# Attention over edges: TensorE adds up the slots of all five groups, and four engines run in a new order

## The chip, the core and the metric

The kernel runs on one core of a Trainium2 chip. The metric is the device time of one execution in microseconds. A core has five engines with queues of their own: TensorE (PE in the profile), VectorE (DVE), ScalarE (ACT), GpSimd (POOL) and SyncE (SP), which here only issues transfers. They meet through semaphores. TensorE adds into PSUM; everything else lies in SBUF.

## What is computed

Four graph layers over 3125 nodes with 16 features and 103125 edges, sorted by their target. Only the fourth, an attention over the edges of each node, is touched:

```python
w_m = (efeat @ W_msg + b_msg).reshape(E, in_f, -1)
w_a = (efeat @ W_attn + b_attn).reshape(E, in_f, -1)
h_src = feat[src][:, :, None]
e1 = w_m * h_src
e2 = w_a * h_src
seg_max = jax.ops.segment_max(e2, dst, num_segments=N)
ex = jnp.exp(e2 - seg_max[dst])
denom = jax.ops.segment_sum(ex, dst, num_segments=N)
attn = ex / denom[dst]
ft = jax.ops.segment_sum(e1 * attn, dst, num_segments=N)
return ft.sum(axis=1)
```

## The kernel before

Edges stand in rows of four slots that share a target node; empty slots are filled. Each of the 128 partitions owns 220 such rows in sequence. Five rows on every partition are five groups, and 5 x 4 = 20 slots are a block (`BLK`); there are 44 blocks (`BLOCKS`). One slot of one block holds, per partition, 512 numbers: for each of 16 input and 16 output features the attention value `e2` and the message `e1`. Two blocks are in flight, in the buffers `e[0]` and `e[1]`, named by `u`.

For each block the work is this. GpSimd gathers the source features of the 20 slots into `hs[u]`, one indirect transfer per slot. TensorE forms one product per slot (line 1872) from the edge features `ef[u]`, which SyncE loads. The product lies in PSUM (`wps`) and is multiplied by the gathered features into `e[u]`: VectorE does slots 0 to 3, 8 to 11 and 16 to 19, four at a time (line 1981), ScalarE slots 4 to 7 and 12 to 15 (line 1942, 16 instructions per slot). VectorE takes the maximum over the four slots of a group (lines 2001 and 2003), carries it from group to group with `up` (line 2010) and back with `down` (line 2015), so that the rows of one node share one shift, and subtracts it (line 2028, one instruction per group). ScalarE takes the exponentials (line 1952, one per group) and that of `scale` (line 1948), the factor by which the state of the block before is rescaled. VectorE weighs the messages with the exponentials (line 2046, one per group). The four slots of a group are then summed: for groups 0 to 3 TensorE adds them with an identity matrix in PSUM (line 1894, four matmuls, eight records in the trace), for group 4 VectorE halves (line 2055) and quarters (line 2060). Then VectorE carries the state over from the block before (line 2067) and accumulates group after group (lines 2081 and 2083). SyncE stores the shifts (line 1785) and the states (line 1790).

The order is written out by hand on each engine. VectorE's `block_step(b)` weighs and accumulates block b - 1, finds the shifts of block b and subtracts them, and multiplies its slots of block b + 1. ScalarE's `turn(b)` multiplies its slots of block b + 1 and takes the exponentials of block b: in the order scale, then groups 4 to 0, all between slots 6 and 7. TensorE's `period` forms the products of block b + 1 between the sums of block b - 1. A turn of ScalarE starts when the gathers of its block have landed and when TensorE has summed group 1 of the block whose buffer it is about to overwrite. TensorE forms a product for ScalarE only when ScalarE has read the one two before, since there are two banks for these, and those for VectorE when the four banks have been read. GpSimd starts the gathers of a block when ScalarE and VectorE have read all of the block two before. ScalarE's loop holds two turns, and the first of the two begins with a table load.

Of the kernel before, what the change touches and what calls it, by code (L numbers as in the profile page):

```python
# [27 lines left out]
F = 16  # L28
# [31 lines left out]
SLOTS = 4  # L60
# [1632 lines left out]
def attention_edges(nc, io, keep, d, sem, lastrow):  # L1693
# [10 lines left out]
    EARLY, LATE1, LATE3 = (4, 5, 6), (7,), (12, 13, 14, 15)  # L1704
    BYACT = [*EARLY, *LATE1, *LATE3]
# [4 lines left out]
    BYPE = 4  # L1710
    SUM_READ = (3, 4, 6, 7)
    SUM_DONE = (2, 2, 3, 4)
    NM = 2
    assert BG == 5 and SLOTS == 4 and sorted(ORDER) == list(range(BLK))
    with ExitStack() as ctx:
        def sb(name, shape, dt=F32):
# [20 lines left out]
        a_w, a_mult, a_read_v, a_read_s, a_sub, a_exp, a_weighed, a_sum, a_halved, a_acc, a_shift, a_last, a_step, a_go = (  # L1737
            sem("a_" + s) for s in "w mult read_v read_s sub exp weighed sum halved acc shift last step go".split())
# [31 lines left out]
        with nc.Block() as block:  # L1770
# [97 lines left out]
            def _(pe):  # L1868
# [20 lines left out]
                def summed(u, b, g):  # L1889

                    pe.wait_ge(a_weighed, b * BYPE + (g + 1))
                    pe.wait_ge(a_acc, b * BG + SUM_READ[g])
                    for c in range(SLOTS):
                        ins = nc.tensor.matmul(sums[:, g % 2, :], ident[:, :], e[u][:, g * SLOTS + c, :],  # L1894
                                               start=(c == 0), stop=(c == SLOTS - 1))
                    ins.then_inc(a_sum, 1)

                def period(u, b, before):
# [17 lines left out]
                    for_dve(u, b, 2, NV + 2)  # L1916
                    for_act(u, b, (13, 14, 15))
# [10 lines left out]
                for g in (1, 0, *range(2, BYPE)):  # L1928
                    summed(0, BLOCKS - 2, g)
                for g in (1, 0):  # L1930
                    summed(1, BLOCKS - 1, g)

            @block.scalar
            def _(act):
# [10 lines left out]
                def exponentials(u, b):  # L1945

                    act.wait_ge(a_sub, b * (BG + 1) + 1)
                    nc.scalar.activation(scale[u][:, :], scale[u][:, :], ACT.Exp).then_inc(a_exp, 1)
                    for n, g in enumerate(reversed(range(BG))):
                        act.wait_ge(a_sub, b * (BG + 1) + (n + 2))  # L1950
                        e2 = all_e2(u, g, g + 1)[:, 0, :, :]
                        nc.scalar.activation(e2, e2, ACT.Exp).then_inc(a_exp, 1)  # L1952
# [3 lines left out]
                multiply(0, 0, [*EARLY, *LATE1])  # L1956
                act.wait_ge(a_first[3], FIRST[3])
                multiply(0, 0, LATE3)
# [14 lines left out]
                exponentials(1, BLOCKS - 1)  # L1973

            @block.vector
            def _(dve):
# [64 lines left out]
                def weigh(v, u, b):  # L2041

                    dve.wait_ge(a_exp, (b + 1) * (BG + 1))
                    for g in range(BG):
                        pair = e[u][:, g * SLOTS:(g + 1) * SLOTS, :].rearrange("p c (i a o) -> p (c i) a o", a=2, o=F)
                        ins = nc.vector.tensor_tensor(pair[:, :, 1, :], pair[:, :, 0, :], pair[:, :, 1, :], ALU.mult)  # L2046
                        if g < BYPE:
                            ins.then_inc(a_weighed, 1)
                        else:
                            v.add(ins)  # L2050
# [12 lines left out]
                def carry(v, u, b, stored):  # L2063

                    dve.wait_ge(a_acc, b * BG + BG)
# [4 lines left out]

                def accumulate(v, u, b, g, by_pe=BYPE):

                    if g < by_pe:
                        total = sums[:, g % 2, :]
                        dve.wait_ge(a_sum, b * BYPE + (BYPE + SUM_DONE[g]))
                    else:
                        total = e[u][:, g * SLOTS, :]
                        v.wait(v.n)
# [10 lines left out]
                dve.sem_inc(a_sum, BYPE)  # L2089
                dve.sem_inc(a_halved, 1)  # L2090
# [21 lines left out]
                largest(v, 0, 0, 0, 3, len(EARLY) + len(LATE1))  # L2112
# [5 lines left out]
                for g in reversed(range(BG)):  # L2118
                    subtract(0, g)
# [4 lines left out]
                def block_step(v, u, b, i, more=True):  # L2124
# [5 lines left out]
                    weigh(v, w, b - 1)  # L2130
                    masks(v, u, b)
# [326 lines left out]
```

## Time and profile before

| | before |
|---|---|
| median of 3 runs | 2714.13 us (2713.15 to 2716.22) |
| profiled execution | 2713.4 us |
| its span, first to last instruction | 2711.7 us |
| VectorE busy | 2260.6 us (83%) |
| TensorE busy, matmuls | 1949.8 us (72%) |
| ScalarE busy | 1747.4 us (64%) |
| GpSimd busy | 1324.2 us (49%) |

The shares are over the whole execution, which has stages with different limits. The attention loop fills the time from about 1116 us to 2643 us; before it lie the other layers, behind it some 70 us in which the rows of each node are fetched and divided. A timeline row gives the start in us from the span's first instruction, the busy time of the instructions merged in it, their number, and in brackets the engine's idle time before them and what ended it. The recorded end of a VectorE instruction lies a little behind the start of the next where that does not depend on it, so costs are read from start to start.

### The profile page before, as it was taken

To read this page: it belongs to the slowest core of one execution; us is meant where nothing else is said; L and a number is where in the kernel's file an instruction comes from. 1 tells how busy PE (TensorE), PEld (TensorE's weight loads), DVE (VectorE), ACT (ScalarE), POOL (GpSimd) and SP (SyncE) were. 2 spreads that over 40 slices of the span, in tenths; PEclk is the share of its full clock that TensorE was granted. 3 is DMA by queue.
4 is the path that set the end of the run, shared out by engine and by line. 5 is a ranking of instruction groups with operands and counts; after the bars stand their busy time and mean duration, and the time that the engine had idled before them with its cause. 6 is when DMAs were issued, how large, how long until landed. Compare 5 with 4: busy or idle time off the path is not lost. (4 is left out here: it accounts for less than half of the span.)

```text
span 2711.7 us, 35345 instructions
## 1 busy us (share of the span) xinstructions
PE 1949.8 (72%) x7015; PEld 998.3 (37%) x7016; DVE 2260.6 (83%) x3915; ACT 1747.4 (64%) x6869; POOL 1324.2 (49%) x1141
## 2 busy tenths in 40 slices
PE   0688888898788978447777777776777777777760
PEld 0344444455444543223333333333333333333320
DVE  7799999313587861269999999999999999999996
ACT  6577777112211112378888888888888888888844
POOL 5000000404551000477777777777777777777705
PEclk8899999887898988668888788888888888888885
DMA  3000000203787652222222223333222332222214
GB/s 71 6 0 0 0 0 0 95 1 120 257 287 240 197 185 71 38 46 85 85 85 85 85 87 89 89 89 87 85 85 85 86 87 86 86 86 86 76 65 118
DMA packets 125233, 238.09 MB, mean 88 GB/s; under 512 B 40438, under 2 KB 68766, under 8 KB 119418
## 3 DMA queue, kind: packets, MB, share of 16 engines
q1 hardware_dynamic: 83289, 189.23, 21.0%
q0 software_dynamic: 41888, 48.19, 8.3%
q8 instruction: 26, 0.43, 0.1%
q14 instruction: 30, 0.24, 0.0%
HBM read 94.14 MB, written 143.02 MB: 87 GB/s over the span
## 5 line engine op out<-in xcount | busy, mean ns | idle before, releaser
L1831 POOL DMA_INDIRECT hs<-h_table,gix x860 | 1084.3, 1261 | 347.3 <-issue 241.8
L1942 ACT ACTIVATE e<-wps,hs 128x32 f32<-128x32 f32 x5632 | 1014.7, 556 | 92.1 <-DMA hs<-h_table,gix 66.6
L1894 PE MATMUL slot_sums<-e,ident 128*128 128x512 f32 x1392 | 773.3, 708 | 18.9 <-DVE states L2081 11.8
L1872 PE MATMUL wps<-w_terms,ef 72*128 72x512 f32 x880 | 409.3, 559 | 451.9 <-ACT e L1942 272.1
L1894 PEld LDWEIGHTS slot_sums<-e,ident 128*128 128x128 f32 x1392 | 318.4, 232 | 395.2 <-issue 362.3
L1872 PEld LDWEIGHTS wps<-w_terms,ef 72*128 72x128 f32 x880 | 178.6, 211 | 643.4 <-ACT e L1942 344.0
L529 ACT CAST edges<-acc 128x400 f32 x600 | 295.2, 492 | 100.1 <-PE acc L516 73.6
L512 PE MATMUL acc<-q_hot,lo_hot 128*128 128x400 bf16 x1200 | 306.6, 337 | 53.7 <-DVE q_hot L486 51.8
L1981 DVE TENSOR_TENSOR e<-wps,hs 128x2048 f32<-128x2048 f32 x132 | 301.9, 2287 | 39.6 <-PE wps L1872 25.6
L554 POOL DMA_INDIRECT got<-in_edge_rows,start x64 | 65.0, 1015 | 543.1 <-POOLq L467 415.9
L486 DVE TENSOR_SCALAR q_hot<-qcol,qT 128x400 bf16<-128x400 bf16 x1200 | 290.8, 321 | 0.3 <-PE acc L516 0.2
L1952 ACT ACTIVATE e<-e 128x1024 f32<-128x1024 f32 x220 | 248.1, 1136 | 55.3 <-DVE e L2028 45.0
L2028 DVE TENSOR_TENSOR e<-e,shifts 128x1024 f32<-128x1024 f32 x220 | 256.8, 1219 | 0.0
L2046 DVE TENSOR_TENSOR e<-e 128x1024 f32<-128x1024 f32 x220 | 253.5, 1220 | 0.0
L1293 PE MATMUL acc<-edges,msg_parts 128*128 128x448 bf16 x1050 | 216.9, 363 | 13.0 <-DMA msg_parts<-msg 13.0
L516 PE MATMUL acc<-edges,ident_b 128*128 x600 | 202.5, 338 | 0.2 <-ACT edges L529 0.2
L1322 ACT CAST efT_high<-tr 128x512 fp32r<-128x512 f32 x56 | 32.8, 586 | 244.2 <-DMA ef_high<-efT_high 201.4
L512 PEld LDWEIGHTS acc<-q_hot,lo_hot 128*128 128x128 bf16 x1200 | 130.8, 140 | 93.6 <-DVE q_hot L486 68.9
L1293 PEld LDWEIGHTS acc<-edges,msg_parts 128*128 128x128 bf16 x1050 | 105.4, 100 | 105.7 <-DMA msg_parts<-msg 13.4
L2001 DVE TENSOR_TENSOR pairs<-e 128x1536 f32<-128x1536 f32 x88 | 130.8, 1487 | 8.3 <-ACT e L1942 8.3
L482 DVE TENSOR_TENSOR lo_hot<-lane,loT 128x1280 bf16<-128x1280 bf16 x120 | 98.7, 823 | 16.1 <-PE acc L516 11.9
L2010 DVE SCALAR_TENSOR_TENSOR shifts<-shifts,mk 128x256 f32<-128x256 f32 x220 | 106.2, 483 | 4.8
(384 smaller groups left out, 2006.7 us busy)
## 6 DMA issues: line engine op xcount, KB each, us to landing
rows_state<-states SPq DMA_DIRECT2D x43, 1280.0 KB, 4.6
rows_shift<-shifts SPq DMA_DIRECT2D x44, 640.0 KB, 3.0
ef<-ef_high SPq DMA_DIRECT2D x88, 180.0 KB
ef<-ef_low SPq DMA_DIRECT2D x88, 180.0 KB
got_order<-edges_order SPq DMA_DIRECT2D x56, 256.0 KB, 2.9
ef_high<-efT_high SPq DMA_DIRECT2D x56, 256.0 KB, 3.1
ef_low<-efT_low SPq DMA_DIRECT2D x56, 256.0 KB, 3.3
hs<-h_table,gix POOLq DMA_INDIRECT x880, 3.8
```

The costliest lines, as they stand in the source:

```text
L486: ins = nc.vector.tensor_scalar(q_hot[:, k % HOTS, s, :], qcol[:, :], qT[:, s, at], None, ALU.is_equal)
L512: nc.tensor.matmul(total, lo_hot[:, k // HOTS % 2, :, k % HOTS * 2 + s], q_hot[:, k % HOTS, s, :], start=(s == 0), stop=False)
L529: nc.scalar.copy(edges[:, :, bass.ds(s16, W)], acc[:, k % BANKS, 0:QW].rearrange("p (t w) -> p t w", w=W)).then_inc(taken, 1)
L1293: ins = nc.tensor.matmul(acc[:, at, 0:CW], parts[:, f, k, a, :], edges[:, k, at * CW:(at + 1) * CW], start=(n == 0), stop=(n == 3 * TILES ...
L1831: nc.gpsimd.indirect_dma_start(out=hs[u][:, s, :], out_offset=None, in_=d["h_table"], in_offset=bass.IndirectOffsetOnAxis(ap=gix[u][:, s:s ...
L1872: nc.tensor.matmul(wps[:, bank, :], ef[u][:, c, g * P:(g + 1) * P], w[:, :], start=True, stop=True).then_inc(a_mult, 1)
L1894: ins = nc.tensor.matmul(sums[:, g % 2, :], ident[:, :], e[u][:, g * SLOTS + c, :], start=(c == 0), stop=(c == SLOTS - 1))
L1942: ins = nc.scalar.mul(e[u][:, s, at], wps[:, bank, at], hs[u][:, s, f:f + 1])
L1952: nc.scalar.activation(e2, e2, ACT.Exp).then_inc(a_exp, 1)
L1981: nc.vector.tensor_tensor(e[u][:, s0:s1, :].rearrange("p s (i c) -> p (s i) c", c=2 * F), wps[:, 0:s1 - s0, :].rearrange("p s (i c) -> p ( ...
L2028: nc.vector.tensor_tensor(e2, e2, bc(shift(u, g), 1, SLOTS), ALU.subtract).then_inc(a_sub, 1)
L2046: ins = nc.vector.tensor_tensor(pair[:, :, 1, :], pair[:, :, 0, :], pair[:, :, 1, :], ALU.mult)
```

## The change

TensorE now sums all five groups of every block but the last, and the halving and quartering on VectorE remain only behind the last block. Groups go in the order 0 to 4 everywhere, where the subtracts and exponentials had gone from 4 to 0. Each weigh waits for its own exponential and not for all six; `scale` has a semaphore of its own (`a_scaled`). VectorE spreads the weighs over the step: 0 and 1, the first maxima, 2, the carry, the second maxima, accumulation 0, weigh 3, the upward shifts, weigh 4. ScalarE takes one exponential at a time between its slots, and scale and groups 3 and 4 after slot 15. The two banks for sums alternate from block to block as well.

```diff
-    ORDER = [4, 5, 0, 1, 2, 3, 6, 7, 8, 9, 10, 11, 12, 16, 17, 18, 19, 13, 14, 15]
+    ORDER = [0, 1, 2, 3, 4, 5, 6, 7, 12, 8, 9, 10, 11, 13, 16, 17, 18, 19, 14, 15]
...
-                    pe.wait_ge(a_weighed, b * BYPE + (g + 1))
-                    pe.wait_ge(a_acc, b * BG + SUM_READ[g])
+                    pe.wait_ge(a_weighed, b * BG + (g + 1))
+                    pe.wait_ge(a_acc, b * BG + (BG + g - 1))
...
+                    for_dve(u, b, 0, NV)
+                    add(0)
+                    for_act(u, b, (4, 5))
                     add(1)
-                    for_act(u, b, (4,))
-                    add(0)
-                    for_act(u, b, (5,))
-                    for_dve(u, b, 0, NV)
+                    add(2)
                     for_act(u, b, (6,))
-                    add(2)
-                    for_act(u, b, (7,))
+                    add(3)
+                    for_act(u, b, (7, 12))
                     for_dve(u, b, 1, NV + 1)
-                    add(3)
-                    for_act(u, b, (12,))
+                    add(4)
+                    for_act(u, b, (13,))
                     for_dve(u, b, 2, NV + 2)
-                    for_act(u, b, (13, 14, 15))
+                    for_act(u, b, (14, 15))
...
-                    act.wait_ge(a_sum, b * BYPE + 1)
-                    multiply(1 - u, b + 1, EARLY)
-                    exponentials(u, b)
-                    multiply(1 - u, b + 1, LATE1)
-                    act.wait_ge(a_sum, b * BYPE + 4)
-                    multiply(1 - u, b + 1, LATE3)
+                    act.wait_ge(a_sum, b * BG + 2)
+                    multiply(1 - u, b + 1, (4, 5, 6))
+                    exponential(u, b, 0)
+                    multiply(1 - u, b + 1, (7,))
+                    act.wait_ge(a_sum, b * BG + 4)
+                    multiply(1 - u, b + 1, (12,))
+                    exponential(u, b, 1)
+                    multiply(1 - u, b + 1, (13,))
+                    exponential(u, b, 2)
+                    multiply(1 - u, b + 1, (14, 15))
+                    rescaled(u, b)
+                    exponential(u, b, 3)
+                    exponential(u, b, 4)
...
+                def weigh(u, b, g):
+
+                    dve.wait_ge(a_exp, b * BG + (g + 1))
...
+                    dve.wait_ge(a_scaled, b + 1)
                     dve.wait_ge(a_acc, b * BG + BG)
...
-                    weigh(v, w, b - 1)
-                    masks(v, u, b)
+                    weigh(w, b - 1, 0)
+                    weigh(w, b - 1, 1)
...
-                    largest(v, u, b, 0, 3, len(EARLY) + len(LATE1))
+                    largest(v, u, b, 0, 3, SLOTS)
+                    weigh(w, b - 1, 2)
+                    carry(v, w, b - 1, i * 16 + 16 * u)
+                    masks(v, u, b)
                     found = largest(v, u, b, 3, BG, NS)
+                    accumulate(v, w, b - 1, 0)
+                    weigh(w, b - 1, 3)
                     v.wait(found)
-                    for g in range(2):
+                    for g in range(4):
                         v.wait(up(v, u, g))
-                    shifted = up(v, u, 2)
-                    halve(w, 4).then_inc(a_halved, 1)
-                    v.wait(shifted)
-                    shifted = up(v, u, 3)
-                    carry(v, w, b - 1, i * 16 + 16 * u)
-                    v.wait(shifted)
                     shifted = up(v, u, 4)
-                    v.wait(shifted - 1)
-                    accumulate(v, w, b - 1, 0)
+                    weigh(w, b - 1, 4)
                     accumulate(v, w, b - 1, 1)
...
+                    subtract(u, 0)
+                    next_block(0)
+                    accumulate(v, w, b - 1, 2)
+                    subtract(u, 1)
+                    subtract(u, 2)
+                    next_block(1)
+                    subtract(u, 3)
+                    accumulate(v, w, b - 1, 3)
                     subtract(u, 4)
-                    next_block(0)
-                    for g in reversed(range(4)):
-                        subtract(u, g)
-                    accumulate(v, w, b - 1, 2)
-                    next_block(1)
-                    dve.wait_ge(a_halved, b + 1)
-                    quarter(v, w, 4)
-                    accumulate(v, w, b - 1, 3)
                     accumulate(v, w, b - 1, 4)
-                    dve.wait_ge(a_acc, b * BG + BG)
                     next_block(2)
```

On VectorE the first half of a step stood like this before (L2046 weighs, L1988 copies the marks, L2001 and L2003 are the maxima, L2010 the upward shifts, L2055 the halving, L2067 the carry, L2081 accumulation 0):

```order
L2046 TENSOR_TENSOR e<-e 128x64x16 x5
L1988 COPY mk<-marks 128x10
L2001 TENSOR_TENSOR pairs<-e 128x1536
L2003 TENSOR_TENSOR shifts<-pairs 128x768
L2001 TENSOR_TENSOR pairs<-e 128x1024
L2003 TENSOR_TENSOR shifts<-pairs 128x512
L2010 SCALAR_TENSOR_TENSOR shifts<-shifts,mk 128x256 x3
L2055 TENSOR_TENSOR e<-e 128x1024
L2010 SCALAR_TENSOR_TENSOR shifts<-shifts,mk 128x256
L2067 TENSOR_TENSOR states<-states,scale 128x512
L2010 SCALAR_TENSOR_TENSOR shifts<-shifts,mk 128x256
L2081 TENSOR_TENSOR states<-states,slot_sums 128x512
```

It now stands like this (L2053 weighs, L2009 and L2011 are the maxima, L2072 the carry, L1996 copies the marks, L2087 is accumulation 0, L2018 the upward shifts):

```order
L2053 TENSOR_TENSOR e<-e 128x64x16 x2
L2009 TENSOR_TENSOR pairs<-e 128x1536
L2011 TENSOR_TENSOR shifts<-pairs 128x768
L2053 TENSOR_TENSOR e<-e 128x64x16
L2072 TENSOR_TENSOR states<-states,scale 128x512
L1996 COPY mk<-marks 128x10
L2009 TENSOR_TENSOR pairs<-e 128x1024
L2011 TENSOR_TENSOR shifts<-pairs 128x512
L2087 TENSOR_TENSOR states<-states,slot_sums 128x512
L2053 TENSOR_TENSOR e<-e 128x64x16
L2018 SCALAR_TENSOR_TENSOR shifts<-shifts,mk 128x256 x5
L2053 TENSOR_TENSOR e<-e 128x64x16
```

The halving is gone, the weighs are apart, the carry has come ahead of the upward shifts, and these stand in one row.

On ScalarE a turn, here the one behind the loop, stood like this before (L1942 multiplies, 16 instructions to a slot, L1948 is the exponential of scale, L1952 that of a group; the last row belongs to what follows the turn):

```order
L1942 ACTIVATE e<-wps,hs 128x32 x48
L1948 ACTIVATE scale<-scale 128x256
L1952 ACTIVATE e<-e 128x64x16 x5
L1942 ACTIVATE e<-wps,hs 128x32 x80
L1948 ACTIVATE scale<-scale 128x256
```

It now stands like this (L1939 multiplies, L1951 is the exponential of a group, L1945 that of scale):

```order
L1939 ACTIVATE e<-wps,hs 128x32 x48
L1951 ACTIVATE e<-e 128x64x16
L1939 ACTIVATE e<-wps,hs 128x32 x32
L1951 ACTIVATE e<-e 128x64x16
L1939 ACTIVATE e<-wps,hs 128x32 x16
L1951 ACTIVATE e<-e 128x64x16
L1939 ACTIVATE e<-wps,hs 128x32 x32
L1945 ACTIVATE scale<-scale 128x256
L1951 ACTIVATE e<-e 128x64x16 x2
```

Scale has moved from behind the third slot to behind the eighth, and two of the five exponentials come after it.

On TensorE a period in the loop began like this before (L1894 is a sum, L1872 a product; the rows without a tile work out what the next one waits for):

```order
L1894 MATMUL slot_sums<-e,ident 128x512 x4
L1886 ISA
L1872 MATMUL wps<-w_terms,ef 128x512
L1891 REGISTER_ALU
L1892 REGISTER_ALU
L1894 MATMUL slot_sums<-e,ident 128x512 x4
L1886 REGISTER_ALU
L1872 MATMUL wps<-w_terms,ef 128x512
L1877 ISA
L1872 MATMUL wps<-w_terms,ef 128x512 x4
```

It now begins like this (L1869 is a product, L1891 a sum):

```order
L1869 MATMUL wps<-w_terms,ef 128x512 x4
L1888 ISA
L1889 REGISTER_ALU
L1891 MATMUL slot_sums<-e,ident 128x512 x4
L1883 ISA
L1869 MATMUL wps<-w_terms,ef 128x512
L1883 REGISTER_ALU
L1869 MATMUL wps<-w_terms,ef 128x512
L1888 REGISTER_ALU
L1889 REGISTER_ALU
L1891 MATMUL slot_sums<-e,ident 128x512 x4
```

Four products for VectorE have come to the front, and two products stand between the first two sums where one stood.

## Rows read from the trace of the kernel before

**Rows 1.** SyncE's queue: the store of the shifts in steps 1 and 43.

```profile
1210.49 0.37 SPq L1785 DMA_DIRECT2D rows_shift<-shifts  x1
...
2617.72 0.33 SPq L1785 DMA_DIRECT2D rows_shift<-shifts  x1
```

**Rows 2.** Busy time in 42 steps: PE, PEld, DVE, ACT, POOL; clock, DMA, GB/s.

```profile
1210.50:2617.70 1407.20, 1012.95 (x2179) 470.79 (x2178) 1385.50 (x1552) 1213.66 (x5612) 1033.07 (x814) 0.82 0.29 84
```

**Rows 3.** Timeline of VectorE in one step: weighs to accumulation 1, then its end.

```profile
1929.68 5.76 DVE L2046 TENSOR_TENSOR e<-e 128x1024 f32<-128x1024 f32 x5
...
1935.43 1.75 DVE L2001 TENSOR_TENSOR pairs<-e 128x1536 f32<-128x1536 f32 x1
...
1938.10 1.22 DVE L2001 TENSOR_TENSOR pairs<-e 128x1024 f32<-128x1024 f32 x1
...
1940.08 1.53 DVE L2010 SCALAR_TENSOR_TENSOR shifts<-shifts,mk 128x256 f32<-128x256 f32 x3
1941.52 1.22 DVE L2055 TENSOR_TENSOR e<-e 128x1024 f32<-128x1024 f32 x1
1942.66 0.48 DVE L2010 SCALAR_TENSOR_TENSOR shifts<-shifts,mk 128x256 f32<-128x256 f32 x1
1943.05 0.68 DVE L2067 TENSOR_TENSOR states<-states,scale 128x512 f32<-128x512 f32 x1
...
1944.05 0.68 DVE L2081 TENSOR_TENSOR states<-states,slot_sums 128x512 f32<-128x512 f32 x1
1944.77 0.75 DVE L2083 SCALAR_TENSOR_TENSOR states<-states,mk,slot_sums 128x512 f32<-128x512 f32 x1
1945.43 2.05 DVE L2015 SCALAR_TENSOR_TENSOR shifts<-shifts,mk 128x256 f32<-128x256 f32 x4
...
1958.65 0.68 DVE L2060 TENSOR_TENSOR e<-e 128x512 f32<-128x512 f32 x1
1959.46 0.75 DVE L2083 SCALAR_TENSOR_TENSOR states<-states,mk,slot_sums 128x512 f32<-128x512 f32 x1
1960.25 0.75 DVE L2083 SCALAR_TENSOR_TENSOR states<-states,mk,e 128x512 f32<-128x512 f32 x1
1961.12 2.29 DVE L1981 TENSOR_TENSOR e<-wps,hs 128x2048 f32<-128x2048 f32 x1
```

**Rows 4.** Timeline of TensorE: first two sums, shortest and longest of 43 pairs.

```profile
1430.15 4.81 PE L1894 MATMUL slot_sums<-e,ident 128*128 128x512 f32 x8
...
1435.03 3.60 PE L1894 MATMUL slot_sums<-e,ident 128*128 128x512 f32 x8
...
2536.02 6.61 PE L1894 MATMUL slot_sums<-e,ident 128*128 128x512 f32 x8
...
2542.70 3.60 PE L1894 MATMUL slot_sums<-e,ident 128*128 128x512 f32 x8
```

**Rows 5.** Timeline of ScalarE: the first turn, and two turns of the loop.

```profile
1181.18 0.80 ACT L1948 ACTIVATE scale<-scale 128x256 f32<-128x256 f32 x1
1181.49 5.21 ACT L1952 ACTIVATE e<-e 128x1024 f32<-128x1024 f32 x5
...
1907.72 1.28 ACT L1942 ACT_TABLE_LOAD   x1 [3.47 <-DMA hs<-h_table,gix]
...
1923.37 14.37 ACT L1942 ACTIVATE e<-wps,hs 128x32 f32<-128x32 f32 x80
1941.12 8.68 ACT L1942 ACTIVATE e<-wps,hs 128x32 f32<-128x32 f32 x48 [3.38 <-DMA hs<-h_table,gix]
```

**Rows 6.** Timeline of GpSimd: a batch of 20 gathers and the next one's first.

```profile
1905.12 1.52 POOL L1831 DMA_INDIRECT hs<-h_table,gix  x1 [2.34 <-ACT e L1942]
...
1926.10 0.94 POOL L1831 DMA_INDIRECT hs<-h_table,gix  x1 [0.30 <-issue]
...
1934.29 1.97 POOL L1831 DMA_INDIRECT hs<-h_table,gix  x1 [0.30 <-issue]
1938.55 1.58 POOL L1831 DMA_INDIRECT hs<-h_table,gix  x1 [2.29 <-ACT e L1942]
```

More of the change, by code:

```diff
@@ L1736, in attention_edges @@
         sums = ctx.enter_context(nc.psum_tensor("slot_sums", [P, 2, 2 * CH], F32))
-        a_w, a_mult, a_read_v, a_read_s, a_sub, a_exp, a_weighed, a_sum, a_halved, a_acc, a_shift, a_last, a_step, a_go = (
-            sem("a_" + s) for s in "w mult read_v read_s sub exp weighed sum halved acc shift last step go".split())
+        a_w, a_mult, a_read_v, a_read_s, a_sub, a_exp, a_scaled, a_weighed, a_sum, a_acc, a_shift, a_last, a_step, a_go = (
+            sem("a_" + s) for s in "w mult read_v read_s sub exp scaled weighed sum acc shift last step go".split())
         a_marks, a_x, a_terms, a_split = sem("a_marks"), sem("a_x"), sem("a_terms"), sem("a_split")
@@ L1927, in _ @@
                         period(u, i * 2 + (2 + u), i * 2 + u)
-                for g in (1, 0, *range(2, BYPE)):
+                for g in range(BG):
                     summed(0, BLOCKS - 2, g)
-                for g in (1, 0):
+                for g in range(BY_PE_LAST):
                     summed(1, BLOCKS - 1, g)
@@ L1943, in multiply, with rescaled, exponential @@
                         ins.then_inc(a_read_s, 1)
-                def exponentials(u, b):
+                def rescaled(u, b):
                     act.wait_ge(a_sub, b * (BG + 1) + 1)
[L1948 to L1952, printed above, removed]
+                    nc.scalar.activation(scale[u][:, :], scale[u][:, :], ACT.Exp).then_inc(a_scaled, 1)
+                def exponential(u, b, g):
+                    act.wait_ge(a_sub, b * (BG + 1) + (g + 2))
+                    e2 = all_e2(u, g, g + 1)[:, 0, :, :]
+                    nc.scalar.activation(e2, e2, ACT.Exp).then_inc(a_exp, 1)
                 act.sem_inc(a_read_s, NS)
                 act.wait_ge(a_first[1], FIRST[1])
-                multiply(0, 0, [*EARLY, *LATE1])
+                multiply(0, 0, (4, 5, 6, 7))
                 act.wait_ge(a_first[3], FIRST[3])
-                multiply(0, 0, LATE3)
+                multiply(0, 0, (12, 13, 14, 15))
                 def turn(u, b, gathered):
                     act.wait_ge(a_gather[1 - u], gathered)
-                    act.wait_ge(a_sum, b * BYPE + 1)
-                    multiply(1 - u, b + 1, EARLY)
-                    exponentials(u, b)
-                    multiply(1 - u, b + 1, LATE1)
-                    act.wait_ge(a_sum, b * BYPE + 4)
-                    multiply(1 - u, b + 1, LATE3)
+                    act.wait_ge(a_sum, b * BG + 2)
[11 more added lines that the diff above has]
+                    exponential(u, b, 4)
                 with act.Fori(0, BLOCKS // 2 - 1) as i:
@@ L1972, in _ @@
                 turn(0, BLOCKS - 2, BLOCKS // 2 * GM)
-                exponentials(1, BLOCKS - 1)
+                rescaled(1, BLOCKS - 1)
+                for g in range(BG):
+                    exponential(1, BLOCKS - 1, g)
             @block.vector
@@ L2039, in group @@
                     return e[u][:, g * SLOTS:(g + 1) * SLOTS, :].rearrange("p c n -> p (c n)")
[L2041 to L2050, printed above, removed]
+                def weigh(u, b, g):
+                    dve.wait_ge(a_exp, b * BG + (g + 1))
+                    pair = e[u][:, g * SLOTS:(g + 1) * SLOTS, :].rearrange("p c (i a o) -> p (c i) a o", a=2, o=F)
+                    nc.vector.tensor_tensor(pair[:, :, 1, :], pair[:, :, 0, :], pair[:, :, 1, :], ALU.mult
+                                            ).then_inc(a_weighed, 1)
                 def halve(u, g):
@@ L2117, in _ @@
                 rescale(0)
-                for g in reversed(range(BG)):
+                for g in range(BG):
                     subtract(0, g)
@@ L2180, in _ @@
                 block_step(v, 1, BLOCKS - 1, BLOCKS // 2 - 1, more=False)
-                weigh(v, 1, BLOCKS - 1)
+                for g in range(BG):
+                    weigh(1, BLOCKS - 1, g)
                 carry(v, 1, BLOCKS - 1, 16 * (BLOCKS // 2))
                 v.wait(v.n)
-                for g in range(2, BG):
+                for g in range(BY_PE_LAST, BG):
                     v.then(halve(1, g))
```

23 lines of the change are left out of this document (10 added, 13 removed).

## The prediction

> **What bounds the kernel now.** The stage that the diff touches is a loop of 44 blocks, one step each on every engine. I read the stores of the shifts first, since SyncE issues one per step: from 1210.49 to 2617.72 us lie 42 steps [rows 1], so a step takes 1407.23 / 42 = 33.51 us, and 42 x 33.51 of the execution's 2713.4 us is this loop. The chain that ended last says nothing here, as it follows only the work behind the loop. Next the busy time of the engines in that stretch [rows 2]: VectorE 1385.5 of 1407.2 us (98.5%), ScalarE 1213.7 (86%), TensorE 1013.0 (72%), GpSimd 1033.1 (73%). Then VectorE's own timeline of one step [rows 3]: no row of it has an idle time before it; each instruction starts where the one before lets it. The others do wait: ScalarE 3.4 us per step for gathered rows [rows 5], GpSimd 2.3 us for ScalarE [rows 6]. So VectorE's sum is the step, and what leaves it is worth its full time until something else is late. How late the others are is the real question.
>
> **Part one: VectorE's step.** Starts are read from the timeline [rows 3]; an instruction that does not wait for the one before starts about 0.08 us before that one's recorded end, one that does wait about 0.03 after.
> The halving of group 4 goes: 1941.52 to 1942.66, 1.14 us. The quartering goes: 0.68 busy, 0.60 by the start-to-start rule.
> The accumulations 3 and 4 each had to wait for their forerunner, 0.79 and 0.87 to the next start; spaced out as they now are, each costs what accumulation 1 costs before the downs, 0.66. That saves 0.13 + 0.21 = 0.34. Accumulation 0 no longer stands right ahead of 1: 0.72 becomes 0.60, 0.12 saved.
> Against this, the five upward shifts now stand in a row. Before, three took 1.44 to the start of the halving, then 0.39 and 0.40 beside other work, 2.23 in all; four dependent ones at 0.52 and one at 0.40 make 2.48, 0.25 more.
> Sum: -1.14 - 0.60 - 0.34 - 0.12 + 0.25 = -1.95. VectorE alone would need 33.51 - 1.95 = 31.56 us. Weighs, subtracts, multiplies, maxima and downs are moved, not changed in number; moving costs nothing as long as VectorE never waits.
>
> **Part two: what VectorE now waits for.** The change turns one wait for six exponentials into one per group, and ScalarE's scale now comes behind slot 15. So I follow one chain, with time 0 at the first weigh of a step. Weigh 0 ends at 1.2; TensorE, which has made products 0 to 3 in that time, starts sum 0 at about 1.3. Sum 0, products 4 and 5 and sum 1 follow. TensorE had the like before, two sums with one product between, in the same place behind a quiet stretch. The shortest such pair in the 43 steps took 1430.15 to 1438.63, 8.48 us, the longest 2536.02 to 2546.30, 10.28 [rows 4]; their middle is 9.4, and a product more costs no more than one of a sum's eight records, 3.60 / 8 = 0.45; I take half of that, 0.23. So sum 1 is there at 1.3 + 9.4 + 0.23 = 10.9. In each pair the first sum is the long one, 4.81 and 6.61 against 3.60: the granted clock averages 0.82 over the stretch [rows 2], and the lower of its two levels falls on the first sum.
> ScalarE's turn starts there, as it must not overwrite slots 4 and 5 before sum 1. In every second turn a table load of 1.28 comes first [rows 5]. Then eight slots at 14.37 / 5 = 2.87 make 23.0, three exponentials at about 1.0 (five in 5.21 where nothing held them) 3.0, the scale 0.31 to the next start. Scaled is there 26.3 later: at 37.2, or 38.5 with the load.
> VectorE wants it at the carry: two weighs at 1.14, the first maximum (1935.43 to 1938.10) 2.67, another weigh 1.14, so 6.1 into the next step, 31.56 + 6.1 = 37.65 on this clock. The plain turn is 0.4 early, the one with the load 0.9 late. Two steps take 2 x 31.56 + 0.9 = 64.0, so a step 32.0. The price of this new wait is bounded below by 0 (TensorE wholly at its higher level, below) and above by the longest pair: sum 1 at 11.8, one turn 1.75 late and the other 0.45, a mean of 1.1 and a step of 32.65. I take 0.45, the middle of the rows.
> Slot 15, which the second maximum needs at 31.56 + 6.9, is read about 0.35 before the scale; that wait comes after the carry and adds nothing once the carry has waited. Exponentials 3 and 4 end 1 and 2 us behind the scale, and weighs 3 and 4 come 3.3 and 7 us behind the carry: covered. Sums 2 to 4 wait for accumulations 0 to 2, and product 6 is queued behind sum 2 on TensorE: sum 2 starts at 10.9, ends near 14.5, and ScalarE wants product 6 at 10.9 + 5.7: covered. Products 8 to 11 and 16 to 19 stand behind sums 3 and 4 only where these are done 2 us ahead of VectorE's multiplies: covered at the higher level; at the lower a multiply waits 1 to 2 us, which happens now and then and is in the upper bound.
>
> **Part three: edges.** The 42 steps give 42 x (33.51 - 32.0) = 63.4 us. In the last step the subtracts and accumulations behind the last store of shifts save the quartering and the waits, 0.9. The first step waits for gathers and ScalarE before and after, which I cost at nothing, plus or minus 1 us. The loads of features still follow product 15, and SyncE's two stores still follow the downs and accumulation 4, in the same order. So 2713.4 - 63.4 - 0.9 = 2649.1. The median of the runs is 0.7 above the profiled execution; I take 2649.
>
> **A rule weighed.** Rows show that after a quiet stretch the first sum takes 4.81 to 6.61 us and the one behind it 3.60 [rows 4]. The Trainium skill (TensorE: Matmul & The Clock Gate, "Part 1: The HAM clock gate") says that the slow clock is the resting state and that activity lifts it. By that rule TensorE's fifth sum could keep the higher level on; the trace agrees that the level rises within the first sum, while whether four more matmuls suffice no row shows.
>
> **Rivals.**
> *VectorE alone.* If both sums ran at the higher level, the pair would take 2 x 3.60 + 2 x 0.23, or 7.7, sum 1 would be there at 9.0 and even the turn with the load would scale at 36.6, before 37.65. The step is 31.56, the time 2713.4 - 42 x 1.95 - 0.9 = 2630.6. For it: more work on TensorE. Against it: no pair of the 43 came near 7.7, and the quiet stretch stays, as products 14 and 15 and then 0 to 3 wait for ScalarE and VectorE.
> *The gathers bind.* A batch of 20 gathers takes 1905.12 to 1936.26, 31.1 us, and the next starts 0.8 after ScalarE's last slot (1923.37 + 14.37 = 1937.74 to 1938.55) [rows 5, 6]; ScalarE gets its rows 4.9 after the last one (1936.26 to 1941.12). One buffer's round trip is thus ScalarE's turn up to slot 15 (26.0, or 27.3 with the load) + 0.8 + batch + 4.9 over two steps. A gather takes 0.94 us, but 1.97 while VectorE weighs [rows 6]; the halving that goes frees one of them, so the batch is 30.2 and the trip 63.2, 31.6 a step: just covered. Were two more gathers of each batch caught by VectorE's newly scattered instructions, the batch would be 32.2 and the step 32.6: 2713.4 - 42 x 0.91 - 0.9 = 2674. The Trainium skill (SBUF — State Buffer, "Who interferes with whom") says that a VectorE instruction with two SBUF inputs blocks a GpSimd instruction that reads SBUF for its whole length; the slow gathers agree. The page infers that making a DMA's descriptors is not caught by it, and there the measured 1.97 decides.
> *Slower.* TensorE at its lower level through both sums: a record at that level takes twice as long, so the pair about 2 x 6.9 + 0.9 = 14.7, sum 1 is there at 16.0, and where both turns bind a step is sum 1 + 26.3 + 0.64 (half the load) - 6.1 = 36.8, 42 x 3.3 = 139 more: 2852. It decides from sum 1 at 12.7, where that sum reaches 33.51, a pair of 11.1. For it: sum 0 follows a quiet stretch. Against: in both pairs shown the second sum is already at 3.60.
> *No gain.* If not VectorE but the gathers' round trip set the step before (31.1 + 4.9 + 30 + 0.8 = 66.8 of 67.0), the halving would be worth nothing: 2713. Against it: the trip is shortened too, as two exponentials and the scale leave ScalarE's turn ahead of slot 15.
>
> **How the numbers follow.** The forecast, a step near 32.0 (2638 to 2660): 0.50. VectorE alone (2628 to 2638): 0.20. Gathers, or TensorE's sums later than the middle (2660 to 2700): 0.22. No gain: 0.03. Slower: 0.05. The range from 2629 to 2674 takes in both ends of the carry's wait and half of the third case, about 0.82. A difference under 0.2%, 5 us, cannot be told from none. Faster 0.92, same 0.03, slower 0.05.
>
> **What would show it.** After: stores of shifts 32.0 apart, in pairs of unequal length; VectorE idle about 0.9 us ahead of the carry in every second step, released by ScalarE's scale, and nowhere else; ScalarE's wait at a turn's start ended by sum 1, no longer by gathers; pairs of sums of 8.5 to 10.5 us. Stores 31.6 apart and no idle time on VectorE mean the first rival; ScalarE still waiting for gathers the second. The prediction is wrong if VectorE waits at a multiply or at a maximum, or if its instructions themselves grow longer.

## The result and the profile after

The changed kernel takes 2664.4 us (median of 4 runs, 2663.5 to 2668.7) against 2715.0 (2713.2 to 2716.2) in runs taken beside it: ratio 0.9817, interval 0.9800 to 0.9834. It is faster, as forecast; the gain is 51 us where 65 were forecast. The time lies inside the range, but not in the band of the forecast (2638 to 2660, chance 0.50); it lies in that of the gathers or of sums later than the middle (2660 to 2700, 0.22). The profiled execution took 2664.25 us, its span 2662.5.

SyncE's stores of the shifts, as in [rows 1]; first the one in step 1, then three in a row, last the one in step 43:

```profile
1210.80 0.37 SPq L1782 DMA_DIRECT2D rows_shift<-shifts  x1
...
1922.49 0.38 SPq L1782 DMA_DIRECT2D rows_shift<-shifts  x1
...
1954.09 0.38 SPq L1782 DMA_DIRECT2D rows_shift<-shifts  x1
...
1987.35 0.38 SPq L1782 DMA_DIRECT2D rows_shift<-shifts  x1
...
2569.39 0.33 SPq L1782 DMA_DIRECT2D rows_shift<-shifts  x1
```

42 steps take 1358.59 us, 32.35 each, where they took 33.51. Short and long steps take turns, 31.60 and 33.26: two steps are 64.86 us, from about 1600 us on without drift. What lies around the 42 steps is 1305.7 us, before 1306.2.

The busy time in these steps, columns as in [rows 2], and then the waits from 1300 to 2500 us (engine, tile, line, what it waited for: us in total, times, longest):

```profile
1210.80:2569.39 1358.59, 1135.74 (x2515) 534.92 (x2514) 1311.48 (x1468) 1192.87 (x5617) 1072.48 (x813) 0.87 0.30 87
```

```profile
ACT L1939 <- PE slot_sums L1891: 83.1, 19, 5.0
...
ACT e L1939 <- DMA hs<-h_table,gix: 49.5, 19, 2.7
...
DVE states L2072 <- ACT scale L1945: 24.7, 19, 1.3
...
POOL hs L1828 <- ACT e L1939: 5.5, 18, 0.3
DVE e L1989 <- PE wps L1869: 2.7, 15, 0.2
```

VectorE's share fell from 98.5% to 96.5%. Its main wait is the carry's, for ScalarE's scale, 1.3 us in every second step; a small one, up to 0.2 us, stands at a multiply (L1989), for TensorE's products. Line L1939 is ScalarE's multiply; its two rows are the two kinds of turn, one with the table load, which sum 1 starts, one without, which waits for gathered rows. GpSimd waits for nothing longer than 0.3 us any more.

VectorE's timeline about the carry of a long step, which begins with a weigh at 1904.09; the first two rows end the step before it, in which the table was loaded:

```profile
1900.89 0.74 DVE L2089 SCALAR_TENSOR_TENSOR states<-states,mk,slot_sums 128x512 f32<-128x512 f32 x1
1901.80 2.29 DVE L1989 TENSOR_TENSOR e<-wps,hs 128x2048 f32<-128x2048 f32 x1 [0.18 <-PE wps L1869]
...
1909.02 1.22 DVE L2053 TENSOR_TENSOR e<-e 128x1024 f32<-128x1024 f32 x1
1911.56 0.69 DVE L2072 TENSOR_TENSOR states<-states,scale 128x512 f32<-128x512 f32 x1 [1.32 <-ACT scale L1945]
```

The carry stands at 7.47 after the first weigh, 1.40 later than in the short step, where it does not wait and stands at 6.07. And the accumulation ahead of the last multiply, of slots 16 to 19, takes 0.91 to the next start (1900.89 to 1901.80), where it takes 0.66 without a wait: 0.25 more, for the products. Together these are the 1.66 us between long and short steps. Then a turn with the load, in the step that begins at 1937.09: first TensorE's rows (products 0 to 3, then sum 0), then ScalarE's (table load, scale):

```profile
1937.14 2.07 PE L1869 MATMUL wps<-w_terms,ef 72*128 72x512 f32 x4 [0.87 <-DVE e L1989]
1939.02 5.88 PE L1891 MATMUL slot_sums<-e,ident 128*128 128x512 f32 x8
```

```profile
1948.91 1.28 ACT L1939 ACT_TABLE_LOAD   x1 [4.36 <-PE slot_sums L1891]
...
1974.83 1.37 ACT L1945 ACTIVATE scale<-scale 128x256 f32<-128x256 f32 x1
```

Sum 0 starts at 1.93, sum 1 lets ScalarE go at 11.8, and scaled is there at 39.1 after the first weigh; the next step begins at 31.85 and wants it 6.07 later, at 37.9.

GpSimd's gathers as a group from 1300 to 2500 us (count, busy us, mean ns of one, idle before), and the longest one:

```profile
L1828 POOL DMA_INDIRECT hs<-h_table,gix x741 | 975.2, 1316 | 225.8 <-issue 220.3 <-ACT e L1939 5.5
```

```profile
1937.85 4.08 POOL L1828 DMA_INDIRECT hs<-h_table,gix  x1 [0.30 <-issue]
```

A gather with the gap before it takes 1.316 + 0.305 = 1.62 us, 20 of them 32.4: the same as the mean step. So there are two suspects for the missing 14 us: the late scale, and GpSimd's full row.

### The profile page after: what moved, and what is told of

Read it like the earlier page. It is cut to its first block and busy times, and to the rows that moved or that the text cites. A ratio compares the mean times of both kernels' runs of the same rounds, so it can differ in the third digit from the quotient of the medians.

```text
span 2662.5 us, 36125 instructions
## 1 busy us (share of the span) xinstructions
PE 2079.0 (78%) x7359; PEld 1067.1 (40%) x7360; DVE 2184.5 (82%) x3829; ACT 1725.0 (65%) x6869; POOL 1365.8 (51%) x1141
## 5 line engine op out<-in xcount | busy, mean ns | idle before, releaser
L1828 POOL DMA_INDIRECT hs<-h_table,gix x860 | 1125.0, 1308 | 263.4 <-issue 257.3
L1939 ACT ACTIVATE e<-wps,hs 128x32 f32<-128x32 f32 x5632 | 1070.8, 681 | 97.8 <-DMA hs<-h_table,gix 49.5
L1891 PE MATMUL slot_sums<-e,ident 128*128 128x512 f32 x1736 | 913.0, 680 | 26.8 <-DVE states L2089 22.6
L1869 PE MATMUL wps<-w_terms,ef 72*128 72x512 f32 x880 | 374.5, 533 | 265.8 <-ACT e L1939 190.8
L1891 PEld LDWEIGHTS slot_sums<-e,ident 128*128 128x128 f32 x1736 | 382.3, 222 | 474.3 <-issue 411.7
L1869 PEld LDWEIGHTS wps<-w_terms,ef 72*128 72x128 f32 x880 | 179.8, 214 | 446.4 <-ACT e L1939 283.4
L1989 DVE TENSOR_TENSOR e<-wps,hs 128x2048 f32<-128x2048 f32 x132 | 301.3, 2283 | 42.4 <-PE wps L1869 39.9
L1951 ACT ACTIVATE e<-e 128x1024 f32<-128x1024 f32 x220 | 322.0, 1629 | 2.3 <-DVE e L2036 2.2
L2053 DVE TENSOR_TENSOR e<-e 128x1024 f32<-128x1024 f32 x220 | 263.9, 1217 | 0.0
L2036 DVE TENSOR_TENSOR e<-e,shifts 128x1024 f32<-128x1024 f32 x220 | 263.5, 1215 | 0.0
L1322 ACT CAST efT_high<-tr 128x512 fp32r<-128x512 f32 x56 | 32.8, 585 | 242.7 <-DMA ef_high<-efT_high 207.5
L2009 DVE TENSOR_TENSOR pairs<-e 128x1536 f32<-128x1536 f32 x88 | 130.6, 1484 | 1.9 <-ACT e L1939 1.9
L2089 DVE SCALAR_TENSOR_TENSOR states<-states,mk,slot_sums 128x512 f32<-128x512 f32 x173 | 127.6, 738 | 0.1
L2018 DVE SCALAR_TENSOR_TENSOR shifts<-shifts,mk 128x256 f32<-128x256 f32 x220 | 106.4, 484 | 6.3
```

Of the source, the lines that this page charges most:

```text
L1828: nc.gpsimd.indirect_dma_start(out=hs[u][:, s, :], out_offset=None, in_=d["h_table"], in_offset=bass.IndirectOffsetOnAxis(ap=gix[u][:, s:s ...
L1869: nc.tensor.matmul(wps[:, bank, :], ef[u][:, c, g * P:(g + 1) * P], w[:, :], start=True, stop=True).then_inc(a_mult, 1)
L1891: ins = nc.tensor.matmul(sums[:, (u + g) % 2, :], ident[:, :], e[u][:, g * SLOTS + c, :], start=(c == 0), stop=(c == SLOTS - 1))
L1939: ins = nc.scalar.mul(e[u][:, s, at], wps[:, bank, at], hs[u][:, s, f:f + 1])
L1989: nc.vector.tensor_tensor(e[u][:, s0:s1, :].rearrange("p s (i c) -> p (s i) c", c=2 * F), wps[:, 0:s1 - s0, :].rearrange("p s (i c) -> p ( ...
L2036: nc.vector.tensor_tensor(e2, e2, bc(shift(u, g), 1, SLOTS), ALU.subtract).then_inc(a_sub, 1)
```

## The experiments

**The load early.** One exponential at the head of ScalarE's loop.

```diff
                 with act.Fori(0, BLOCKS // 2 - 1) as i:
+                    nc.scalar.activation(early[:, :], ident[:, 0:1], ACT.Exp)
                     turn(0, i * 2, i * GM + GM)
```

> The changed kernel, with one exponential of a column of the identity matrix put at the top of ScalarE's loop, ahead of its waits, so that the loop's table load is over before sum 1 is there. Theory (the scale comes 1.4 to 1.66 us late to the carry in every second step, because of the 1.28 us load that stands behind the wait for sum 1): the load lies in the 4.36 us in which ScalarE waits anyway, the scale ends about 1.28 earlier, at 5.97 instead of 7.25 after the step's start, against 6.07 at which VectorE wants it. The long steps of 33.25 shrink to 31.6 to 31.8, the short ones stay at 31.59: 2664 - 20 x 1.5 = about 2634 us (2629 to 2640). Rival one (GpSimd's gathers, back to back, set the pace): no change, 2660 to 2666. Rival two (the low TensorE clock over sums 0 and 1 makes the lateness by itself): part of it, 2645 to 2655.

Measured: 2678.0 us, ratio 0.9857 (0.9832 to 0.9882), 14 us above the change (11 us by the two ratios). All three expectations missed. Waits and gathers:

```profile
ACT e L1940 <- DMA hs<-h_table,gix: 149.1, 37, 5.4
...
DVE states L2074 <- ACT scale L1946: 37.4, 34, 1.7
```

```profile
L1829 POOL DMA_INDIRECT hs<-h_table,gix x733 | 977.5, 1334 | 223.4 <-issue 217.6 <-ACT e L1940 5.8
```

Nearly every ScalarE turn now waits for gathered rows, and a step is 32.70 us: 20 x (1.334 + 0.305) = 32.8. With the load out of the way GpSimd's row is the bound, and it is longer than the 32.35 of the change.

**The kernel before with the load early**, the same line.

> The kernel before with the same early table load. Theory (VectorE's own row of work sets the 33.51 us step there, and ScalarE has room for its load): no change, 2712 to 2717 us. Rival (ScalarE's late exponentials already held VectorE before, so that the change gained by another way than VectorE's shorter row): a gain of 0.3 to 0.6 us in each step or in every second one, 2690 to 2707 us.

Measured: 2716.2 us, ratio 0.9997 (0.9987 to 1.0006): no change. ScalarE did not hold the step before.

**Halving back on VectorE**, the new orders kept.

```diff
-                    add(4)
...
+                    dve.wait_ge(a_weighed, b * BG)
+                    halved = v.add(halve(w, 4))
...
+                    quarter(v, w, 4)
                     accumulate(v, w, b - 1, 3)
```

> The changed kernel with its new orders kept, but group 4 halved and quartered on VectorE again, TensorE summing four groups. Theory (the gain comes from VectorE's work that was taken away, 1.14 + 0.60 us and the waits that stand with it, and the new order only makes room for it): the step is 31.59 + 1.74 + about 0.2 = 33.4 to 33.6 us without a wait for the scale, since VectorE wants it at the same point of its row while ScalarE has 1.8 us more: 42 x (33.5 - 32.42) more than the 2664 of the change, about 2709 us (2700 to 2716). Rival (the gain is the order's, the interleaved exponentials): 2660 to 2675 us.

Measured: 2719.8 us, ratio 1.0013 (1.0004 to 1.0023). Its 42 steps:

```profile
1216.46:2626.64 1410.18, 1032.59 (x2178) 492.86 (x2177) 1386.51 (x1552) 1193.94 (x5604) 972.55 (x813) 0.76 0.31 84
```

A step is 33.58 us and VectorE waits for none of the others, so all of the gain comes from the work taken off VectorE; the new orders alone give 33.58 a step against 33.51. The expected time was low: it set the step at 33.5 and the change's at 32.42, where 33.58 and 32.35 were measured (6 us), and it left out what lies ahead of the store in step 1, which comes 5.7 us later than in the change.

**Sixteen gathers.** This kernel leaves out four gathers of each block, so it does not do the whole computation; the same holds for all kernels below with 16 or 19.

```diff
+        GATHERED = (*range(4, BLK),)
...
-                    for s in range(BLK):
+                    for s in GATHERED:
...
+                    h0 = 8 if n == 0 and (not isinstance(b, int) or b > 0) else s0
...
-                        bc(hs[u][:, s0:s1, :].rearrange("p s i -> p (s i)"), 2, 2 * F), ALU.mult
+                        bc(hs[u][:, h0:h0 + 4, :].rearrange("p s i -> p (s i)"), 2, 2 * F), ALU.mult
```

> The changed kernel with 16 of 20 row gathers in every block: slots 0 to 3 are not gathered, and VectorE multiplies their products by the rows of slots 8 to 11 instead, so its work and its reads keep their size but the values of these slots are others. Theory (gathers don't set the pace, though GpSimd has no idle time left): the long steps stay at about 33.2, 2655 to 2666 us. Rival (the gathers, up to 4.08 us long now and without a pause between blocks, set the pace of the long steps): 2630 to 2645 us.

Measured: 2660.4 us, ratio 0.9797 (0.9781 to 0.9813). The 42 steps take 1358.84 us, as in the change; what is gained lies ahead of the first store, which comes at 1205.17 instead of 1210.80. Waits and gathers:

```profile
ACT L1940 <- PE slot_sums L1892: 96.3, 18, 5.4
...
ACT e L1940 <- PE slot_sums L1892: 40.4, 19, 2.2
...
DVE states L2074 <- ACT scale L1946: 25.7, 19, 1.4
```

```profile
L1829 POOL DMA_INDIRECT hs<-h_table,gix x591 | 716.3, 1212 | 484.6 <-ACT e L1940 308.1 <-issue 176.5
```

GpSimd has idle time again and ScalarE waits for sums alone, yet the carry waits as before: the late scale is enough by itself for 32.35 us a step.

**Both at once, and nineteen gathers with the load early.** The first is the load's line and the sixteen gathers together; the second differs from it by these (and `h0` is 1):

```diff
-        GATHERED = (*range(4, BLK),)
+        GATHERED = (*range(1, BLK),)
```

> The changed kernel with the early table load and 16 of 20 gathers in every block at once (slots 0 to 3 are not gathered and take the rows of slots 8 to 11, as in the kernel with sixteen gathers). New theory (two bounds stand within half a per cent of each other: ScalarE's late scale, which alone gives 64.86 us for two steps, and GpSimd's row of 20 gathers, 20 x (1.32 to 1.33 + 0.30) = 32.4 to 32.8 us a block, which alone gives 65 us and more): with both gone, VectorE's own row of 31.59 us is left in every step, with at most 0.1 for the scale, 2664 - 42 x (32.42 - 31.65) = 2632 us (2626 to 2640). Rival (the early load itself costs, or a third bound such as TensorE's clock stands behind both): 2650 us or more.

Measured: 2632.1 us, ratio 0.9677 (0.9661 to 0.9693). Its stores of the shifts in steps 1 and 43, and VectorE's one wait:

```profile
1205.70 0.37 SPq L1784 DMA_DIRECT2D rows_shift<-shifts  x1
...
2536.81 0.33 SPq L1784 DMA_DIRECT2D rows_shift<-shifts  x1
```

```profile
DVE states L2076 <- ACT scale L1947: 2.0, 5, 0.4
```

31.69 us a step: VectorE alone, but for these few waits. Neither edit gained in the loop by itself; together they take the time 32 us below the change's. That the forecast of 2632 was hit so closely is in part luck: it counted on 32 us in the loop, which gave 42 x (32.35 - 31.69) = 28, and the other 5 came from ahead of the store in step 1 (1205.70 instead of 1210.80).

> As the one before, but with 19 of 20 gathers: only slot 0 is not gathered, and slots 0 to 3 are multiplied by the rows of slots 1 to 4. New theory (GpSimd's back-to-back row sets the pace where the load is early): 19 x 1.64 = 31.1 us is less than VectorE's 31.59, so one gather fewer is enough and the time is 2630 to 2645 us. Rival (it is not the row's length but the lateness of what starts a block's gathers, so one fewer takes off one gather's 1.6 us at most once): 2655 to 2675 us.

Measured: 2639.6 us, ratio 0.9706 (0.9690 to 0.9722), 31.73 us a step. One gather fewer in each block is enough, which says that the length of GpSimd's row is what binds once the load is early.

**The scale sooner**, with 20 gathers and with 16.

```diff
-                    multiply(1 - u, b + 1, (14, 15))
                     rescaled(u, b)
+                    multiply(1 - u, b + 1, (14, 15))
```

> The changed kernel with the exponential of the scale moved ahead of ScalarE's multiplies of slots 14 and 15, all 20 gathers kept, load where it was. New theory (two bounds): the scale comes some 5.7 us sooner and the wait at the carry goes; the second maxima now wait for slots 14 and 15, about 0.5 later than the row wants them in the turn with the load, and the gathers stay at 32.4 us or more a block: 2660 to 2680 us, no gain. Rival (the late scale alone sets the pace): two steps 63.2 to 64.2, 2637 to 2658 us.

Measured: 2670.5 us, ratio 0.9823 (0.9805 to 0.9841), no gain. The carry's wait is gone; these stand in its place:

```profile
ACT L1939 <- DMA hs<-h_table,gix: 74.6, 16, 5.1
...
ACT e L1939 <- DMA hs<-h_table,gix: 30.6, 10, 3.3
...
DVE pairs L2009 <- ACT e L1939: 12.7, 19, 0.9
DVE e L1989 <- PE wps L1869: 11.1, 12, 1.4
```

> The changed kernel with 16 of 20 gathers (slots 0 to 3 take the rows of slots 8 to 11) and the exponential of the scale ahead of ScalarE's multiplies of slots 14 and 15, load where it was. With 20 gathers this order gained nothing (2670). Theory (there GpSimd's row of gathers held the pace, which is shown by ScalarE's turns that waited up to 5.1 us for gathers): with 16 the order gains, the carry no longer waits, and only the second maxima wait up to 0.9 us for slots 14 and 15 in every second step: two steps 63.2 to 64.1, 2632 to 2650 us. Rival (the early scale costs as much at the second maxima as it gains at the carry): 2655 to 2670.

Measured: 2632.9 us, ratio 0.9693 (0.9677 to 0.9709), 31.79 us a step. So a second, different way to get the scale in time gives the same: nothing with 20 gathers, VectorE's pace with 16.

**Why two steps take 64.86 us.** The next four ask what sets the lateness of the scale, all with 16 gathers.

```diff
+                        if n == 2:
+                            product(u, s, s - s0, count=False)
+                            product(u, s, s - s0, count=False)
                         product(u, s, s - s0)
```

> The changed kernel with 16 of 20 gathers (as in the kernel with sixteen gathers) and each product of slots 16 to 19 computed three times into the same bank, so that TensorE is busier late in each step. It asks how much of the late scale, the only bound left with sixteen gathers (64.86 us for two steps), is the TensorE clock. Theory (in the turn with the load, products 0 to 3 and sums 0 and 1 run partly at the low level, which makes sum 1 end at 11.7 after the step's start where 10.9 was expected): with the clock higher there, sum 1 ends at 10.9 to 11.2, the scale comes 0.5 to 0.8 sooner, two steps take 64.0 to 64.4: 2660 - 20 x 0.5 to 0.8 = 2644 to 2650 us. Rival (sum 1 is late by VectorE's weighing, not by the clock): 2657 to 2663 us. The extra products could also hold up slots 14 and 15: then slower than 2663.

Measured: 2664.1 us, ratio 0.9799 (0.9782 to 0.9815), just above the rival's range.

```profile
DVE e L1996 <- PE wps L1870: 22.1, 19, 1.2
DVE states L2079 <- ACT scale L1951: 5.7, 18, 0.3
```

The scale did come about 1 us sooner to the carry, but the extra products made VectorE's last multiply wait 1.2 us: the steps are 32.01 and 32.85, together again 64.86. A gain on one wait and a loss on another that cancel to the hundredth were odd enough to test the sum itself.

```diff
                     act.wait_ge(a_sum, b * BG + 2)
+                    if u == 0:
+                        for n in range(2):
+                            nc.scalar.activation(early[:, n:n + 1], ident[:, n:n + 1], ACT.Exp)
```

> The changed kernel with 16 of 20 gathers and two exponentials of one column (0.20 us each) behind the wait for sum 1 in every second ScalarE turn, the one with the table load. It asks whether the 64.86 us of two steps, which three kernels with different waits now show, is the sum of a chain. Theory one (a chain: sum 1, load, turn, scale, carry, and from the carry on all of the next two steps): 0.41 us more in the chain are 0.41 us more for two steps, 65.27 us, 2660 + 20 x 0.41 = 2668 us (2666 to 2671). Theory two (the two steps have settled on the rhythm in which TensorE's granted clock falls and rises, and the chain gives way within it): 64.8 to 64.9 us, 2659 to 2663 us.

Measured: 2631.4 us, ratio 0.9686 (0.9670 to 0.9702), outside both expectations. ScalarE's timeline says why:

```profile
2113.86 3.04 ACT L1953 ACTIVATE e<-e 128x1024 f32<-128x1024 f32 x2
2116.92 1.28 ACT L1966 ACT_TABLE_LOAD   x1
2120.10 0.30 ACT L1966 ACTIVATE early<-ident 128x1 f32<-128x1 f32 x2 [1.89 <-PE slot_sums L1893]
```

The load now stands ahead of the wait for sum 1, so this run added nothing to the chain: it hid the load, as the first experiment did, with the same result as in the run with both edits. The question went to two runs that add multiplies, two and five, which leave the load in place.

```diff
                     multiply(1 - u, b + 1, (14, 15))
+                    if u == 0:
+                        for n in range(2):
+                            nc.scalar.mul(small[:, n:n + 1], ident[:, n:n + 1], ident[:, n:n + 1])
                     rescaled(u, b)
```

> The changed kernel with 16 of 20 gathers and, in every second ScalarE turn, the one with the table load, two multiplies of one column (about 0.18 us each) just ahead of the scale's exponential. The load stays where it was, unlike with the two exponentials. Theory one (the 64.86 us of two steps are the sum of a chain through the scale): two steps 65.2 us, 2667 us (2665 to 2670). Theory two (the two steps have settled on TensorE's rhythm): 64.8 to 64.9 us, 2659 to 2663 us.

Measured: 2661.6 us, ratio 0.9798 (0.9782 to 0.9814).

> As the one before, with five multiplies of one column, about 0.9 us. Theory one (a chain): two steps 65.8 us, 2679 us (2674 to 2684). Theory two (TensorE's rhythm): 64.8 to 64.9 us as long as the rhythm holds, 2659 to 2665 us.

Measured: 2664.2 us, ratio 0.9817 (0.9801 to 0.9833). The table load with two and with five multiplies, in steps that begin at 1934.79 and 1936.57, and the five multiplies with the scale behind them:

```profile
1946.14 1.28 ACT L1941 ACT_TABLE_LOAD   x1 [5.01 <-PE slot_sums L1893]
```

```profile
1947.43 1.28 ACT L1941 ACT_TABLE_LOAD   x1 [3.99 <-PE slot_sums L1893]
```

```profile
1973.30 2.03 ACT L1975 ACTIVATE small<-ident 128x1 f32<-128x1 f32 x5
1974.23 1.40 ACT L1947 ACTIVATE scale<-scale 128x256 f32<-128x256 f32 x1
```

Work of 0.37 and 0.93 us ahead of the scale (start to start) added nothing to the pair; with five multiplies the pairs swing between 64.6 and 65.0 us late in the loop, and their mean is still 64.86. Sum 1 came earlier by nearly as much: the load starts 11.73 after the step's start with none, 11.35 with two, 10.86 with five. TensorE's clock in that step, 4 to 8 us after its start with no multiply added, 4 to 6 with two, 4 to 8 with five (window, its length, PE busy, granted clock, DMA share, GB/s):

```profile
2065.40:2067.40 2.00, 2.00 (x3) 0.50 0.59 119
2067.40:2069.40 2.00, 2.00 (x6) 0.92 0.62 135
```

```profile
1938.79:1940.79 2.00, 2.00 (x4) 0.61 0.61 127
```

```profile
1940.57:1942.57 2.00, 2.00 (x5) 0.86 0.59 119
1942.57:1944.57 2.00, 2.00 (x6) 1.00 0.61 136
```

The low level (0.50, 1.2 GHz) ends earlier in the step where the chain behind it is longer: worked out from the means in these rows, at 6.32 us without, 5.56 with two and 4.56 with five. At 0.50 half as much is done in a microsecond as at 1.00, so 0.76 and 1.76 us less of it should bring sum 1 about 0.4 and 0.9 us sooner, an estimate from these rows that fits the load's starts. So the pair of steps settles where the low level delays sum 1 just enough, and its 64.86 us is not the sum of the chain's parts. That the clock is the cause is read from these rows; no run took its changes away.

No kernel that does the whole computation was faster than the change.

## Why the prediction held, and where it was off

- **VectorE is the bound before:** right; hiding the load there gave 0.9997.
- **Part one, 31.56 us for VectorE alone:** right. The short steps are 31.60 and the run with both other bounds away 31.69 a step. Undoing it lost the whole gain.
- **Part two, which wait is next:** right in place, engine and rhythm: the carry, for the scale, only after turns with the load. Two of the prediction's signs came out against it: VectorE also waits at a multiply, and ScalarE's turns without the load are still ended by gathered rows (49.5 us in 19 turns), though these did not set the pace.
- **Part two, the size:** this step failed. Two steps take 64.86 us where 64.0 were forecast, and 42 x (32.35 - 32.0) = 14.7 us is nearly the whole miss. Two terms were too small. The turn with "the load 0.9 late" is 1.40 late at the carry. The multiplies' wait for products 16 to 19, which the sum put at nothing, as one that "happens now and then", measured 0.25 in the steps with the load: sum 4, ahead of these products, began at 1960.17 with the granted clock at 0.57 over its first 4 us and took 5.29 us, where sums at the high level take 3.60.
- **Why the scale was later:** From sum 1 on the working held: from load to scaled 27.3 us, 27.6 in the prediction. Ahead of it sum 0 started at 1.93 instead of 1.3, since products 0 to 3 ran at the low level too (2.07 us for four), and sum 1 let ScalarE go at 11.8 instead of 10.9. I took the middle of pairs that drift from 8.48 to 10.28 us [rows 4]. In the kernel before they drift because VectorE's fixed step slides past the clock's changes. These are the stretches from 10 to 13 us after the first weigh in four steps in a row (window, its length, PE busy, granted clock, DMA share, GB/s):

```profile
1332.12:1335.12 3.00, 3.00 (x7) 0.75 0.64 140
1365.62:1368.62 3.00, 3.00 (x7) 0.65 0.63 144
1399.12:1402.12 3.00, 3.00 (x5) 0.54 0.62 147
1432.62:1435.62 3.00, 3.00 (x9) 1.00 0.63 145
```

  The first sum took 5.61, 5.88, 6.24 and 4.81 us in them. In the change the slide stops once the chain through sum 1 sets the step: from 4 to 7 us after the first weigh of three steps with a load in a row (from 1941.09, 2005.94 and 2070.79) the granted clock is 0.58 each time. So one late place is taken for good, and the middle of the drift says nothing of where that is. The 0.75 us that the waits cost per step lies inside the bounds of 0 to 1.1.
- **Part three:** the edges gave 0.5, forecast 0.9.
- **The rule weighed:** the level did not stay high. In long and short steps alike the granted clock is down to 0.50 by 2 us after the start and is back at 1.00 before sum 1 is done. The Trainium skill (TensorE: Matmul & The Clock Gate, "Part 1: The HAM clock gate") says that activity lifts the level; the trace agrees, as the clock is 0.50 up to 1943.08 and 1.00 from 1945.08 us while the sums run. Four more matmuls a step did not keep it up, though the mean over the 42 steps is 0.87, against 0.76 in the same order with four sums.
- **Rivals:** VectorE alone (2630.6) is what remains with load and gathers out of the way: 2632.1, of which 5 us were won ahead of the loop. The gathers (2674) did not bind in the change, where 16 instead of 20 moved nothing in the loop, but stood right behind: they gave 2678.0 once the load was hidden and 2670.5 once the scale came sooner. I had the batch shrink to 30.2 us; it grew to 32.4, as a gather became longer, from a mean of 1.267 to 1.316 us.

## What to carry to other kernels

When the bound engine's row is cut, work out every other engine's full row as well as its waits: here two bounds stood within about 1% of each other, so either alone could be removed without gain, and only the pair of edits showed it. Don't size a new wait by the middle of a spread that came from a loop with another bound; a loop that waits for an engine with changing clock can settle at one place of it. And look at the trace for where a table load stands before counting on an edit near it.

## What the runs showed of the hardware

- Kernels with four different chains (no addition, extra products, two and five extra multiplies) settled at the same 64.86 us for two steps on average, and up to 0.93 us of added work on the waiting chain was free.
- GpSimd's gathers depend on what VectorE does meanwhile. In the change, from 1300 to 2500 us, all 185 that began beside a multiply, which reads one input from PSUM, took 0.94 or 0.95 us; the 148 that began beside a weigh, which reads both from SBUF, took 1.90 in the mean and up to 4.08. The mean of all was 1.18 us in the run with both edits, 1.32 in the change, 1.33 with the load early.
- The 1.28 us table load stood behind the wait for sum 1 where a multiply is first in the loop, and ahead of that wait where an exponential is. I suppose that it follows which wait is attached to the first instruction that needs the table; that was not tried apart.
